# A graph network's edge expansions in halves, with the third layer's lane numbers stored as 8-bit integers

## The reference

```python
# second layer (L1): graph convolution
h = features * (deg_out ** (-0.5))[:, None] @ weight
rst = jax.ops.segment_sum(h[src], dst, num_segments=n_nodes)
rst = rst * (deg_in ** (-0.5))[:, None] + bias
# third layer (L2): messages with edge attributes
msg = jax.nn.relu(x[src] + edge_attr)
agg = jax.ops.segment_sum(msg, dst, num_segments=x.shape[0])
```

## Time and profile before

| | |
|---|---|
| median of three runs | 8933.99 us (8924.55 to 8934.04) |
| profiled execution | 8922.76 us |
| its span, first to last instruction | 8920.1 us |
| TensorE, VectorE, ScalarE, POOL busy | 71%, 66%, 28%, 55% |
| bytes moved by DMA | 1295.50 MB, mean 145 GB/s |
| expansion of layer two | 3133 to 3894 us |
| sum by target of layer two | 3894 to 4830 us |
| expansion of layer three | 4914 to 5594 us |

### The profile page before, as it was taken

How to read it: one execution, slowest core, us unless ns; L and a number is a source line. 1 busy time by engine, 2 the same in 40 slices (tenths; PEclk the granted TensorE clock), 3 DMA queues, 4 the chain that set the end, 5 groups by cost and what they waited for, 6 DMA issues and landing times. The chain is left out here.

```text
span 8920.1 us, 183726 instructions
## 1 busy us (share of the span) xinstructions
PE 6289.7 (71%) x35446; PEld 4927.1 (55%) x35447; DVE 5909.6 (66%) x18166; ACT 2529.7 (28%) x8033; POOL 4865.1 (55%) x4975
## 2 busy tenths in 40 slices
PE   2688888888847645556664555788668888888886
PEld 1577777777735433345553222566456666666664
DVE  8566666666669755568887888899554444444444
ACT  5355555555511222211110222111112221222222
POOL 0477777777756200047773000677347777777773
PEclk9555555555555655568886555999855555555556
DMA  6655555454546399987786999666633333333333
GB/s 133 152 154 149 156 148 154 149 156 147 156 97 139 72 190 195 195 198 224 230 226 130 246 257 257 181 181 178 92 111 82 80 80 80 81 81 80 82 80 30
DMA packets 1822628, 1295.50 MB, mean 145 GB/s; under 512 B 1262870, under 2 KB 1643574, under 8 KB 1820576
## 3 DMA queue, kind: packets, MB, share of 16 engines
q1 hardware_dynamic: 1580112, 841.10, 39.9%
q0 software_dynamic: 200704, 415.20, 17.9%
q10 hardware_dynamic: 40912, 29.67, 1.5%
HBM read 923.76 MB, written 361.78 MB: 144 GB/s over the span
## 5 line engine op out<-in xcount | busy, mean ns | idle before, releaser
L1138 POOL DMA_INDIRECT sorted_edges<-arena,idx x1664 | 1619.0, 973 | 727.8 <-issue 638.7
L2253 POOL DMA_INDIRECT arena<-node_table,idx x1760 | 1660.4, 943 | 557.0 <-issue 388.9
L1053 PE MATMUL banks<-arena,edge_tables 128*128 x3520 | 1164.7, 439 | 288.3 <-DVE edge_tables L982 233.8
L2229 PE MATMUL banks<-arena 128*128 128x64 f32 x3520 | 1214.1, 448 | 0.0
L1639 PE MATMUL banks<-arena 128*128 x3520 | 670.9, 361 | 769.2 <-issue 435.2
L1053 PEld LDWEIGHTS banks<-arena,edge_tables 128*128 128x128 f32 x3520 | 898.5, 317 | 417.6 <-issue 393.3
L2224 PE MATMUL banks<-arena 128*64 128x65 f32 x3520 | 843.0, 343 | 401.0 <-ACT arena L2240 400.3
L2128 POOL DMA_INDIRECT arena<-expanded,idx x576 | 544.6, 945 | 1003.5 <-DVE idx L2005 788.5
L2229 PEld LDWEIGHTS banks<-arena 128*128 128x128 f32 x3520 | 883.4, 311 | 210.2
L2240 ACT ACTIVATE arena<-arena 128x64 f32<-128x64 f32 x1760 | 450.1, 257 | 1787.2 <-DVE arena L2192 1781.6
L2199 DVE TENSOR_TENSOR arena<-arena,banks 128x64 f32 x1760 | 387.8, 220 | 820.2 <-PE banks L2229 792.8
(11 more groups left out here) (426 smaller groups left out, 11712.5 us busy)
## 6 DMA issues: line engine op xcount, KB each, us to landing
arena<-sorted_edges SPq DMA_DIRECT2D x220, 524.0 KB
arena<-lanes_dram SPq DMA_DIRECT2D x222, 512.0 KB, 8.0
expanded<-arena SPq DMA_DIRECT2D x110, 784.0 KB, 8.0
arena<-in_attr_rows SPq DMA_DIRECT2D x576, 130.0 KB
arena<-sorted_edges SPq DMA_DIRECT2D x110, 536.0 KB
arena<-row_keys SPq DMA_DIRECT2D x110, 512.0 KB
arena<-sorted_edges SPq DMA_DIRECT2D x110, 512.0 KB, 5.6
expanded<-arena SPq DMA_DIRECT2D x110, 512.0 KB
```

The source lines that it names most:

```text
L1053: nc.tensor.matmul(m.psum[j % 4][:, 0:D], m.onehot[:, j % 4, :], m.support[:, bass.ds(blocks[j] * D, D)], start=True, stop=True).then_inc( ...
L1138: nc.gpsimd.indirect_dma_start(m.sorted, bass.IndirectOffsetOnAxis(ap=m.idx[:, j % (4 * CH):j % (4 * CH) + 1], axis=0), m.out_ring[:, slot ...
L2229: nc.tensor.matmul(m.psum[j % 4][:, 0:D], m.onehot8[:, c % 4, j % CB, :], row[:, 0:D], start=True, stop=True).then_inc(s["summed"], 1)
L2253: nc.gpsimd.indirect_dma_start(slots[:, j % SLOTS, 0:D], None, m.table, bass.IndirectOffsetOnAxis(ap=m.idx[:, j % SLOTS:j % SLOTS + 1], ax ...
```

## The change

Both expansions work in halves of a chunk (eight tiles, four PSUM banks) in place of quarters, with one load of 16 block numbers per chunk ahead of the wait for `turned`. In layer two ScalarE copies both halves, after VectorE's `take` of that half; VectorE's `put` goes. A row of layer two is 112 floats for 98, the pad set to 0 once; the target stands at column 97 as before. In layer three the lanes come from a second store, `lanes8_dram`, as 8-bit integers; SP broadcasts 2048 bytes per partition for 4096, and ScalarE widens them to bf16 (`widen`) two chunks ahead, for two buffers that `turn` reads. SP asks for the next lanes once they are widened. One of the two one-hot buffers for attributes in layer two's sum lies elsewhere. The core of the diff:

```diff
-ROW2 = PARTS // 2 + 2
+ROW2 = 112
+COUNT2 = PARTS // 2
+DST2 = COUNT2 + 1
...
+    m.lane_rows8 = arena[:, at:at + 5 * SB * P // 4].bitcast(I8).rearrange("p (c t) -> p c t", c=5)
+    m.wide_rows = arena[:, at + 5 * SB * P // 4:at + 9 * SB * P // 4].bitcast(BF16).rearrange("p (c t) -> p c t", c=2)
...
+    m.lanes8_dram = dram("lanes8_dram", (TSX * P,), I8)
...
                     a.activation(lane_rows[:, n:n + size], m.psum[n // QUAD][:, 0:size], ACT.Copy).then_inc(s["lanes_out"], 1)
+                    a.activation(lane_rows8[:, n:n + size], m.psum[n // QUAD][:, 0:size], ACT.Copy).then_inc(s["lanes_out"], 1)
...
-                sp.wait_ge(s["lanes_out"], -(-TSX // QUAD))
-                sp.dma_start(m.lanes_dram.rearrange("(k t p) -> t k p", t=P, p=P), lane_rows.rearrange("t (k p) -> t k p", p=P)
-                             ).then_inc(s["stored"], 16)
-                sp.wait_ge(s["stored"], 16)
+                sp.wait_ge(s["lanes_out"], 2 * -(-TSX // QUAD))
+                for to, rows in ((m.lanes_dram, lane_rows), (m.lanes8_dram, lane_rows8)):
+                    sp.dma_start(to.rearrange("(k t p) -> t k p", t=P, p=P), rows.rearrange("t (k p) -> t k p", p=P)
+                                 ).then_inc(s["stored"], 16)
+                sp.wait_ge(s["stored"], 32)
...
+        lane_rows, lanes_dram = (m.lane_rows, m.lanes_dram) if layer == 2 else (m.lane_rows8, m.lanes8_dram)
...
                 if layer == 2:
-                    sp.wait_ge(s["put_act"], n * 2 + 2 + 2)
-                    sp.wait_ge(s["put_dve"], n * 2 + 2 + 2)
+                    sp.wait_ge(s["put"], n * 2 + 2 + 2)
                     sp.wait_ge(s["dst"], n + 1)
                 else:
-                    sp.wait_ge(s["row"], n * 4 + 4)
+                    sp.wait_ge(s["row"], n * 2 + 2)
...
-                    sp.wait_ge(s["turned"], n + 1)
+                    sp.wait_ge(s["turned" if layer == 2 else "wide"], n + 1)
...
+                v.memset(out16[:, :, :, PARTS + 4:2 * ROW2].rearrange("p c t f -> p (c t) f"), 0.0).then_inc(s["blank"], 1)
...
-                dve.wait_ge(lanes_in[c % 5], i * (chunks // 5 * 16) + c // 5 * 16 + 16)
-
-                dve.wait_ge(s["expanded"], n * 4 + 4)
-                v.tensor_scalar(m.turned16[:, c % 2, :], m.lane_rows[:, c % 5, :], m.lane_no[:, :], None, ALU.is_equal
+                if layer == 2:
+                    dve.wait_ge(lanes_in[c % 5], i * (chunks // 5 * 16) + c // 5 * 16 + 16)
+                else:
+                    dve.wait_ge(s["wide"], n + 1)
+                lanes = lane_rows[:, c % 5, :] if layer == 2 else m.wide_rows[:, c % 2, :]
+
+                dve.wait_ge(s["expanded"], n * 2 + 2)
+                v.tensor_scalar(m.turned16[:, c % 2, :], lanes, m.lane_no[:, :], None, ALU.is_equal
...
+            def take(i, c, h):
                 n = i * chunks + c
+                dve.wait_ge(s["expanded"], n * 2 + h + 1 + 2 * 2)
...
-            def put(i, c, u):
-                n = i * chunks + c
-                dve.wait_ge(s["expanded"], n * 4 + u + 1 + 2 * 4)
-                to = rows_of(out16, c, u)[:, :, :, 0:PARTS]
-                v.tensor_copy(to, quad[:, 2 * u:2 * u + 2, 0:2 * PARTS].rearrange("p k (t f) -> p k t f", f=PARTS)).then_inc(s["put_dve"], 1)
-                take(i, c, u)
...
+                to, attr = half_of(out, c, h), half_of(m.attr_rows, c, h)
+                v.tensor_tensor(to, sum_of(h, 0), attr, ALU.add).then_inc(s["summed"], 1)
...
+                    numbers = run_values(nc, ENG.PE, m.sorted_block[:, bass.ds(n * SB, SB)], NB)
                     pe.wait_ge(s["turned"], n + 1)
-                    for u in range(4):
-                        k = n * 4 + u
-                        if u % 2 == 0:
-                            numbers = run_values(nc, ENG.PE, m.sorted_block[:, bass.ds(n * SB + 4 * u, 8)], NB)
...
+                    for h in range(2):
                         if layer == 3:
+                            pe.wait_ge(s["added"], n * 2 + h + 1)
                         else:
+                            pe.wait_ge(s["put"], n * 2 + h + 1)
+                            pe.wait_ge(s["taken"], n * 2 + h + 1)
                         settle(pe)
+                        for j in range(HALF):
+                            t = HALF * h + j
...
+            def widen(i, c):
+                n = i * chunks + c
+                act.wait_ge(lanes_in[c % 5], i * (chunks // 5 * 16) + c // 5 * 16 + 16)
+                if not (isinstance(n, int) and n < 2):
+                    act.wait_ge(s["turned"], n - 1)
+                a.activation(m.wide_rows[:, c % 2, :], lane_rows[:, c % 5, :], ACT.Copy).then_inc(s["wide"], 1)
+
+            def body(i, first, last):
                 for c in range(chunks):
                     n = i * chunks + c
+                    if layer == 3 and not (last and c == chunks - 1):
+                        widen(i, c + 2)
...
+                    for h in range(2):
                         if layer == 3:
+                            act.wait_ge(s["added"], n * 2 + h + 1 + 2)
+                            rows = out[:, c % 5, HALF * h:HALF * h + HALF, :]
                             a.activation(rows, rows, ACT.Relu).then_inc(s["row"], 1)
+                        else:
+                            act.wait_ge(s["expanded"], n * 2 + h + 1 + 2 * 2)
+                            act.wait_ge(s["taken"], n * 2 + h + 1 + 2)
+                            a.activation(half_of(out16, c, h)[:, :, :, 0:PARTS],
+                                         quad[:, 4 * h:4 * h + 4, 0:2 * PARTS].rearrange("p k (t f) -> p k t f", f=PARTS),
+                                         ACT.Copy).then_inc(s["put"], 1)
```

More of the change, by code:

```diff
@@ L9 @@
 I16 = mybir.dt.int16
+I8 = mybir.dt.int8
 ALU = mybir.AluOpType
@@ L167, in allocate @@
     at += SB * P
+    assert ROW2 * 5 * SB <= 10 * SB * D and DST2 < ROW2
     m.row_out = arena[:, at:at + 5 * SB * ROW2].rearrange("p (c t f) -> p c t f", c=5, f=ROW2)
@@ L184, in allocate @@
     at += SB * P
[L185 to L186 removed]
+    assert at <= ARENA
     at = NB * PARTS
@@ L226, in allocate @@
     assert AIMED * 3 <= TD
-    m.onehot_attr = [part.bitcast(BF16).rearrange("p (f s) -> p f s", s=CB) for part in (attr_onehot, tables[:, free:free + CB * P // 2])]
+    m.onehot_attr = [part.bitcast(BF16).rearrange("p (f s) -> p f s", s=CB) for part in (tables[:, 4 * TP:4 * TP + CB * P // 2], tables[:, free:free + CB * P // 2])]
     m.attr_parts = [tables[:, TSX + n * PARTS:TSX + (n + 1) * PARTS] for n in range(2)]
@@ L1452, in _ @@
             def _(sp):
-                sp.wait_ge(s["lanes_out"], -(-TSX // QUAD))
-                sp.dma_start(m.lanes_dram.rearrange("(k t p) -> t k p", t=P, p=P), lane_rows.rearrange("t (k p) -> t k p", p=P)
-                             ).then_inc(s["stored"], 16)
-                sp.wait_ge(s["stored"], 16)
+                sp.wait_ge(s["lanes_out"], 2 * -(-TSX // QUAD))
[3 more added lines that the diff above has]
+                sp.wait_ge(s["stored"], 32)
 def expand_by_source(nc, m, layer):
     with ExitStack() as ctx:
-        s = sems(nc, "blank", "turned", "expanded", "put_act", "put_dve", "dst", "summed", "added", "row", "reached", "found", "taken", "zeros")
+        s = sems(nc, "blank", "turned", "expanded", "put", "dst", "summed", "added", "row", "reached", "found", "taken", "zeros", "wide")
         lanes_in = ring(nc, "lanes_in", 5)
@@ L1599, in body @@
                         reach(i, c)
-                    if not first or c >= 5:
+                    if layer == 3 and (not first or c >= 5):
                         dve.wait_ge(stored[c % 5], i * (chunks // 5 * 16) + c // 5 * 16)
-                    for u in range(4):
+                    for h in range(2):
                         if layer == 3:
-                            add(i, c, u)
-                        elif u % 2:
-                            put(i, c, u)
+                            add(i, c, h)
+                        else:
+                            take(i, c, h)
             body(0, True)
@@ L1637, in _ @@
                         settle(pe)
-                        for j in range(4):
-                            done = nc.tensor.matmul(quad[:, 2 * u + j // 2, j % 2 * PARTS:(j % 2 + 1) * PARTS],
-                                                    m.turned16[:, c % 2, (4 * u + j) * P:(4 * u + j + 1) * P],
-                                                    parts[:, bass.ds(numbers[4 * (u % 2) + j] * PARTS, PARTS)], start=True, stop=True)
-                        if layer == 2 and u % 2:
+                        for j in range(HALF):
+                            t = HALF * h + j
+                            done = nc.tensor.matmul(quad[:, t // 2, t % 2 * PARTS:(t % 2 + 1) * PARTS],
+                                                    m.turned16[:, c % 2, t * P:(t + 1) * P],
+                                                    parts[:, bass.ds(numbers[t] * PARTS, PARTS)], start=True, stop=True)
```

(10 more changed lines are left out.)

72 lines of the change are left out of this document (26 added, 46 removed).

## The result

The changed kernel takes 8778.2 us (median of 4, 8770.0 to 8783.3) where the kernel before takes 8932.7 beside it (median of 4): ratio 0.9828, 95% interval 0.9811 to 0.9845, or -154.5 us. The forecast was -214, 8720. The profiled execution took 8776.9 us around a span of 8775.1.

What follows compares the result with a forecast made beforehand. Layer two was taken as bound by the TensorE-VectorE-TensorE loop, layer three by the DMA. -138 (layer two) - 95 (layer three) + 3.5 + 3 + 12 = -214 us, giving 8720 at the median; range 8640 to 8920.

Steps and rivals of the forecast that it cites:

- rival C: Layer three: 8-bit lanes do not shorten the DMA, broadcast is paid per packet; period stays 6.06, 8814 us; chance 0.10.
- the loop set 6.76: Layer two before the change: the loop TensorE, VectorE, TensorE sets the 6.76 us a chunk, the DMA close behind.
- The DMA's 5.5: Layer two's new period by DMA: store 3.2, lanes 2.0, plus 0.3 to 0.4, taken as 5.5 us a chunk; -138 us.
- TensorE's 5.2: Layer two's new period by TensorE: load of 16 about 1.10 and the rest of the chunk 4.1, 5.2 us.
- Rival B: Both expansions: the load of 16 is disturbed in every chunk, periods 6.45 and 5.35, 8840 us; chance 0.15.
- Rivals A and D: Layer two's wider store: A, today's stall stays, 7.3 us, chance 0.15; D, stalled from its first packet, 8.56, chance 0.07.
- here the DMA bounds: Layer three before the change: the DMA sets 6.06 us a chunk, VectorE 7% behind; with the change 5.2, -95 us.
- VectorE's 4.77: Layer three's new period by VectorE alone, with halves: 4.10 + 0.67 = 4.77 us, against 5.64.
- The 0.38 unexplained: Layer three's DMA before: store and attributes 3.65 plus lanes 2.03 make 5.68; 0.38 us was missing to 6.06.
- the 1 us that was named as the sign: Layer three: half-size lanes passing in about 1 us would show the forecast; 2 us would show rival C.
- The cover of the widening: Layer three: VectorE's work was to cover ScalarE's 1.9 us widening; a turn waiting for it would mean the cover is gone.
- The sum by target: Layer two's sum: gathers move 14% more bytes; a tenth of the 119.5 us wait for attribute rows, +12 us.

Runs made afterwards that it cites:

- e_before112: The kernel before with layer two's rows at 112 floats and the one-hot buffer moved, old engine lists kept: 8953.1 us, beside 8928.7 for the kernel before.
- e_l2_noload: The changed kernel without layer two's register load per chunk, four fixed block numbers used instead (wrong blocks multiplied): 8709.9 us, beside 8928.7 for the kernel before.
- e_rows98: The changed kernel with layer two's rows at 98 floats (392 bytes) again, no pad: 8986.3 us, beside 9007.6 for the kernel before.
- e_l3_attr_act: The changed kernel with layer three's attribute fetch asked for by ScalarE in place of SP: 8704.8 us, 0.9658 of the kernel before.
- e_l2_split_load: e_l3_attr_act with layer two's 16 block numbers loaded in two loads of eight, one before each half: 8783.7 us, beside 9011.8 for the kernel before.

## Why the prediction was right, and where not

The sign, and the time within its range, were right; by its steps it was part luck. The range was stretched to 8920 us for the rivals, so it held a layer three that moved by 3%, though "either period stays put" was to show the forecast wrong; 8778 lies nearer to rival C's 8814 than to the forecast's 8720.

- **Layer two, -163.8 for -138.** Right in mechanism: the loop set 6.76 (e_before112), the store was close behind, and 448-byte rows keep their pace at 628 to 680 packets per us (637 forecast). The bound of the new period was wrong. The DMA's 5.5 was too long: it sustains 4.73 (e_l2_noload). TensorE's 5.2 was too short: its load took 1.47 for 1.10, the rest of its chunk 3.85 for 4.1. So TensorE and not the DMA sets the 5.32, and that it lies near 5.5 is luck.
- **Rival B** was half right: the load is slowed in every chunk, but to 1.47, not 2.35. Rivals A and D are out by the packets' pace; what they feared is what 392-byte rows do (e_rows98).
- **Layer three, -19.6 for -92.** The step that failed is "here the DMA bounds". VectorE's wait for lanes asked for five chunks ahead showed that the lanes came late; it didn't show that the packets were slow. They were asked for late, in the kernel before 6.1 us ahead in place of five chunks, by a queue that stood at its issues. With SP relieved, VectorE's 4.77 came out as forecast (4.75), and TensorE's load is 1.11 there, so those terms were right and hidden behind a bound I hadn't read.
- **The 0.38 unexplained** in the sum 5.68 was the warning: a sum of packet rates that closes to 6% is no proof. SP's own 2.12 + 0.39 + 2.66 + 0.9 closes as well.
- **Rival C** gave the right period for a wrong reason. The lanes do not pay per packet at the DMA: a packet of them took 206 ns before and 115 after (medians, 5000 to 5300 us). But their issue waits out the store ahead of it, and spread among the other packets the 128 pass in 2.6 us for 2.8, not in the 1 us that was named as the sign.
- **The cover of the widening** went as feared: VectorE waits for it 122 us over layer three (L1569, groups by line), because ScalarE waits for its lanes 319 us. Its own 1.91 is as forecast.
- **The sum by target, +24.9 for +12:** the term was half of it. All of it is the wait for attribute rows. e_before112 has +26 with the rows and the moved one-hot buffer; e_rows98, with that buffer and the old width, lies 15 to 24 us below the others of its chip, so most is the width's. With sums of one code 18 us apart on a chip (1053.0, 1071.0), its size is not known better.
- **Ahead of layer two:** copies and second store +3.2 of the +5.0 (from the first copy of the lanes to the blank row's store, 5.8 before and 9.0 after), forecast +3.5.
- **Layer three's sum, +8.0,** has no edit in it. e_l2_noload, with the changed layer three ahead of it, has 968.5 there, so I take it for spread between executions; its cause wasn't looked for.

Both kernels are beaten by e_l3_attr_act, 0.9658 of the kernel before against 0.9828 for the change.

## What to carry to other kernels

Before calling a stretch DMA-bound, read the issuing engine's queue: if its issues fill the period, and what they bring is asked for hardly ahead of its use, let another engine ask for one of the transfers. Smaller packets gave 26 to 32 us here, the other queue some 39 in the kernel before and 112 to 121 in the changed one. Two bounds that lie about 2% apart hide each other: a change that moves one of them shows nothing until the other moves too. A store whose rows fall from their first pace was worth padding here, to 416 or 448 bytes, and the reader of those rows pays for the pad.

## What the runs showed of the hardware

- An issue on SP takes 0.39 to 0.40 us behind a transfer of 128 packets. Right behind one of 2048 on the same queue it takes 2.0 to 4.2 us in layer three, and in layer two 1.4 us (e_l2_split_load) to 5.8 us, behind 392-byte rows (e_rows98); all are medians of a run.
- A register load of 16 takes 1.11 to 1.12 us (medians) where the store's packets stall (e_rows98) or in e_l3_attr_act's layer three, 1.34 in the change's layer three, 1.47 beside 448-byte stores, 1.80 when POOL asks for the lanes there. What slows it stays open.
- 392-byte rows back to back fall to 403 packets per us; 416-byte rows hold, 677 per us in a window of the same length (3459.5 to 3460.5) and 653 from 3460.6 to 3461.6:

```profile
DMA packets 677, 0.29 MB, mean 288 GB/s; under 512 B 675, under 2 KB 675, under 8 KB 677
```
